# Six windowed attention layers on one NeuronCore: an inverse and a normalization placed earlier in the round

## What is computed

```python
def attn_layer(x, Wqkv, qs, ksc, Wo):              # 16 heads of 64, windows of 32
    q, k, v = split(x @ Wqkv)
    q = l2norm(q) * qs;  k = l2norm(k) * ksc       # row norms: 1/sqrt(sum of squares)
    q = q*cos*scale + rotate_half(q)*sin*scale
    k = k*cos/scale + rotate_half(k)*sin/scale
    attn = softmax(mask(8.0 * q @ k2.T), -1)       # k2, v2: this window and the one before
    return (attn @ v2) @ Wo
for i in range(6):
    x = attn_layer(shift_tokens(x), ...) + x
    x = ffn_layer(shift_tokens(x), ...) + x        # layer norm, gelu gate, two products
```

## Time and profile before

| what | value |
|---|---|
| median of 3 runs (lowest, highest) | 2273.87 us (2270.52, 2282.59) |
| span of the profiled execution, which is its own time here | 2279.7 us |
| TensorE busy | 2005.6 us, 88% |
| VectorE busy | 1815.6 us, 80% |
| ScalarE busy | 1660.3 us, 73% |
| GpSimd busy | 1267.3 us, 56% |

### The profile page before, as it was taken

How to read it: one execution, slowest core, us unless ns; L and a number is a source line. 1 busy time by engine, 2 the same in 40 slices (tenths; PEclk the granted TensorE clock), 3 DMA queues, 4 the chain that set the end, 5 groups by cost and what they waited for, 6 DMA issues and landing times. The chain is left out here.

```text
span 2279.7 us, 55457 instructions
## 1 busy us (share of the span) xinstructions
PE 2005.6 (88%) x20349; PEld 1350.3 (59%) x20349; DVE 1815.6 (80%) x3618; ACT 1660.3 (73%) x3144; POOL 1267.3 (56%) x1132
## 2 busy tenths in 40 slices
PE   5788888689999999999999999999999999985274
PEld 3333333356766776776676767677667767764153
DVE  4666663699999999999999999999999999944633
ACT  2255556378888888888888888888888888874123
POOL 4400000577677777767767766776776776731052
PEclk8699998799999999999999999999999999997587
DMA  6311100111111121111211112111211111100512
GB/s 159 101 42 44 23 2 11 58 36 38 30 39 29 35 82 29 39 29 39 78 29 39 30 41 75 31 37 30 87 30 29 39 30 38 30 29 26 188 34 68
DMA packets 70562, 107.36 MB, mean 47 GB/s; under 512 B 20887, under 2 KB 47774, under 8 KB 68734
## 3 DMA queue, kind: packets, MB, share of 16 engines
q1 hardware_dynamic: 68262, 100.87, 15.4%
q0 software_dynamic: 1280, 2.62, 0.4%
q10 hardware_dynamic: 752, 0.33, 0.1%
HBM read 41.60 MB, written 12.26 MB: 24 GB/s over the span
## 5 line engine op out<-in xcount | busy, mean ns | idle before, releaser
L1583 POOL TENSOR_TENSOR qk<-rot_cos,rot_sin 128x512 f32<-128x512 f32 x256 | 323.2, 1273 | 154.6 <-DVE rot_sin L1361 154.6
L1593 POOL TENSOR_TENSOR qk<-qk,rnorm 128x512 f32<-128x512 f32 x256 | 263.1, 1043 | 88.0 <-DVE rnorm L1394 88.0
L1359 DVE TENSOR_TENSOR rot_cos<-pA,layer_tab 128x512 f32<-128x512 f32 x384 | 263.2, 685 | 60.1 <-ACT sq L1171 55.1
L434 ACT ACTIVATE probs_by_key<-pT 128x512 f32<-128x512 f32 (+3 forms) x384 | 177.1, 490 | 155.4 <-PE pT L320 121.0
L499 DVE TENSOR_REDUCE minus_max<-pS 128x1 f32<-128x1024 f32 (+7 forms) x256 | 184.6, 754 | 110.0 <-PE pS L290 109.2
L1171 ACT ACTIVATE sq<-pA 128x512 f32<-128x512 f32 x384 | 228.5, 595 | 53.1 <-PE pA L890 43.6
L1371 DVE TENSOR_REDUCE sumsq<-sq 128x8 f32<-128x512 f32 x384 | 253.6, 671 | 14.3 <-ACT sq L1171 14.2
L1361 DVE TENSOR_TENSOR rot_sin<-pA,layer_tab 128x512 f32<-128x512 f32 x384 | 261.1, 680 | 0.0
L1231 ACT ACTIVATE probsT<-pD 64x512 f32<-64x512 f32 x380 | 224.0, 589 | 35.3 <-PE pD L931 31.9
L1600 POOL TENSOR_TENSOR probs<-probs,row_inverse 128x1024 f32<-128x1024 f32 x96 | 182.6, 1903 | 100.3 <-DVE row_inverse L1430 100.3
L1191 ACT ACTIVATE qT<-pC 64x512 f32<-64x512 f32 x384 | 225.9, 588 | 7.3 <-PE pC L905 0.5
(11 more groups left out here) (342 smaller groups left out, 4659.0 us busy)
## 6 DMA issues: line engine op xcount, KB each, us to landing
v_shifted<-v SPq DMA_DIRECT2D x96, 384.0 KB, 3.5
v_shifted<-v SPq DMA_DIRECT2D x95, 128.0 KB, 3.4
q_stack<-stacked SPq DMA_DIRECT2D x24, 192.0 KB
k_stack<-stacked SPq DMA_DIRECT2D x24, 192.0 KB
W_ahead<-in_Wqkv_dram SPq DMA_DIRECT2D x12, 384.0 KB
layer_weights<-in_Wqkv_dram SPq DMA_DIRECT2D x12, 384.0 KB
stacked<-part SPq DMA_DIRECT2D x32, 128.0 KB, 2.4
tokens_in<-tokens SPq DMA_DIRECT2D x2, 1024.0 KB
```

The lines of the kernel that those rows point to most:

```text
L1359: dve.tensor_tensor(t1[c % 2][:, :].rearrange("p (h g d) -> p h g d", g=2, d=32), a, tabl[s % 2][:, j].unsqueeze(1).broadcast_to([P, 8, 2, ...
L1583: pool.tensor_tensor(qk(s, c), t1[c % 2][:, :], t2[c % 2][:, :], ALU.add).then_inc(added[c], 1)
L1593: pool.tensor_tensor(v, v, rn[p % 2][:, o:o + 8].unsqueeze(2).broadcast_to([P, 8, DH]), ALU.mult).then_inc(scaled[c], 1)
```

## The change

Two calls move in the hand-written lists. In `dve_body`, `rec(r - 2, 1)` moves from behind `ss(2, r, 1)` to directly behind `sum_(r - 2, 1)`. In `pool_body`, `norm(r - 2, 1)` moves from behind the last two sums of the round's second tile to ahead of them, and those two sums swap places.

```diff
@@ dve_body
             rec(r - 2, 0)
             ss(0, r, 1)
             sum_(r - 2, 1)
+            rec(r - 2, 1)
             ss(1, r, 1)
             rot(1, r, 1)
             rot(2, r, 1)
             ss(2, r, 1)
-            rec(r - 2, 1)
             ya(r - 3)
             ss(3, r, 1)
             nw(r)
@@ pool_body
             norm(r - 2, 0)
             add(0, r, 1)
+            norm(r - 2, 1)
+            add(1, r, 1)
             add(2, r, 1)
-            add(1, r, 1)
-            norm(r - 2, 1)
             sc(1, r, 0)
```

## The result

The changed kernel took 2210.28 us (median of 4 runs, 2202.35 to 2220.80); the kernel before, with one more run, 2272.19 us (2270.23 to 2282.59). The ratio is 0.972, 95% interval 0.967 to 0.976: faster by 62 us, where 50 were forecast. The direction and the mechanism held; the gain was a quarter larger than forecast.

A forecast was written before the change was run, and what follows sets the result against it. Each round was taken as closed by a loop through TensorE, ScalarE and VectorE, with Newton held by GpSimd. 45 rounds x 1.10 us = 49.5 us, with the third round 50 us together: median 2273.87 to 2224 us, range 2209 to 2255.

The forecast's parts named there:

- The overlap with the normalization: VectorE's first Newton instruction is held while GpSimd's second normalization runs: 1.92 us instead of 0.23, 1.69 us a round.
- GpSimd's new chain: GpSimd runs normalization, sum of chunk 0, second normalization, sums of chunks 1 and 2 in succession, ending at 1255.1.
- the 0.8 us of margin: Time between GpSimd going quiet and the start of Newton on VectorE, 0.8 us.
- 0.27 us for the reciprocal's new place: Directly behind its sum the reciprocal delays `ss` and `rot` of chunk 1 by 0.27 us, covered by later idle time.
- What the 1.69 us are worth: Step turning VectorE's saving into round time: TensorE's idle time 0.96 plus 0.14 us, 1.10 us a round.
- My 0.14 us: Share counted of TensorE's 0.23 us wait at a V projection's weight load, a little over half.
- the 0.73 of the prediction: Part of VectorE's 1.69 us that exceeds TensorE's 0.96 us idle time ahead of `W2` and becomes margin, 0.73 us.
- 1 us for the third round: The third round loses its own 1.6 us but gets a new overlap with a sum; about 1 us of gain left.
- Longer waits of VectorE for squares: Sign of being right: VectorE's waits for squares, 1.03 and 0.31 us a round before, grow with TensorE as the bound.
- the first rival: GpSimd's last sum runs into Newton and holds it instead of the normalization; 0.42 us a round remain, 2255; chance 0.10.
- the second: Rival: VectorE was the only bound, so the full 1.69 us a round is gained, 2198; chance 0.04.
- the third or fourth: Rivals: TensorE stops for another wait, 2249 to 2274, chance 0.12; the moved reciprocal delays what follows, 2286, chance 0.05.

## Why the prediction was wrong in size

**What held.** The overlap with the normalization, its 1.69 us, and that it goes (1.924 to 0.226 us); GpSimd's new chain and the 0.8 us of margin; no cost for the other order of the sums; 0.27 us for the reciprocal's new place, fully covered. TensorE as the bound afterwards.

**The step that failed** is "What the 1.69 us are worth": "0.96 + 0.14 = 1.10 us". The measured value is 1.54 us. TensorE's own list takes 31.85 us, and I had taken 32.43 us of its round for work, from its busy time: the limit was the right one and its size was wrong. TensorE's timeline of the kernel before, at the end of a round:

```profile
1261.37 0.44 PE L964 MATMUL pD<-ident,x_feature_major 128*128 128x128 f32 x2
1261.78 1.12 PE L896 MATMUL pA<-layer_weights,x_feature_major 128*128 128x512 f32 x2
1262.75 1.02 PE L890 MATMUL pA<-layer_weights,x_feature_major 128*128 128x512 f32 x2
1263.67 0.63 PE L905 MATMUL pC<-ident,tokens 128*128 128x128 f32 x4
1264.14 1.02 PE L890 MATMUL pA<-layer_weights,x_feature_major 128*128 128x512 f32 x2
1265.00 0.60 PE L905 MATMUL pC<-ident,tokens 128*128 128x128 f32 x4
1266.56 0.67 PE L1062 MATMUL pE<-ff_midT,W_ahead 128*128 128x256 f32 x2 [0.96 <-DVE ff_midT L1474]
```

and of the changed one:

```profile
1200.84 0.44 PE L964 MATMUL pD<-ident,x_feature_major 128*128 128x128 f32 x2
1201.12 1.02 PE L896 MATMUL pA<-W_ahead,x_feature_major 128*128 128x512 f32 x2
1201.98 1.02 PE L890 MATMUL pA<-layer_weights,x_feature_major 128*128 128x512 f32 x2
1202.83 0.60 PE L905 MATMUL pC<-ident,qk 128*128 128x128 f32 x4
1203.27 1.02 PE L890 MATMUL pA<-layer_weights,x_feature_major 128*128 128x512 f32 x2
1204.13 0.60 PE L905 MATMUL pC<-ident,qk 128*128 128x128 f32 x4
1204.57 1.46 PE L1062 MATMUL pE<-ff_midT,W_ahead 128*128 128x256 f32 x6
```

From start to start, before and after: last transposes to `W2` 1.56 and 0.44 us, so this wait was 1.12 us, not 0.96. The recorded duration of four transposes, 0.60 us, is longer than the 0.44 us after which TensorE takes the next thing, and it hid 0.16 us of the wait. `L1` to V projection 0.41 and 0.28; V to Q projection 0.97 and 0.86; Q projection to transposes 0.92 and 0.85; transposes to Q projection 0.47 and 0.44. That is 0.34 us in four steps that the profile calls busy. My 0.14 us stood for the first of them, the V projection's wait (0.13); I had put the rest at nothing. `W2` took 1.37 us until the next transposes started (from 1233.17 to 1234.54 in the same timeline), and takes 1.30 now (from 1204.57 to 1205.87). Together 1.12 + 0.34 + 0.07 = 1.53 us. Much of it could be read before: elsewhere in the old round four transposes are followed after 0.44 us, a Q projection after 0.86 and six matmuls like `W2`'s (L977) after 1.30, and I had not compared them. For the step from the V to the Q projection it could not: the old round shows 0.96 us at its other place too, and why 0.86 is reached now stays open, as it does for `L1`, which has no second place. With less slack than I took, the margin of VectorE came out at 0.19 us and not at the 0.73 of the prediction.

**Two smaller terms.** 43 full rounds at 1.54 us are 66 us; the earlier, shorter rounds and the few longer ones give the other 4 us (forecast 1 us for the third round). Against that stand the several us by which the start of a run scatters, which I had not considered beyond 5 us. That 2210.28 us lies 1 us inside the range of 2209 to 2255 is luck of this kind: two of the four runs took 2202 and 2203 us, and the 70.5 us that the layers gave would make 2202. Of the four only the one at 2217.59 us has a trace, so for the others the start is not shown.

**Signs that I named.** Rounds of 32.3 us: wrong, 31.85. A busy share near 99%: 100%. Longer waits of VectorE for squares: wrong; they are 0.80 and 0.41 us against 1.03 and 0.31, since the round shrank by nearly all that VectorE gave up; my argument against the first rival, that they grow, fails with it. **The rivals:** the first occurred only in the third round of the changed kernel, the 0.617 us in its source line; the second was nearly right, 1.54 of 1.69 us, at a chance of 0.04 that was too low because it rested on the same 32.43 us; nothing of the third or fourth.

## What to carry to other kernels

A small VectorE instruction that takes several times as long as its siblings and ends together with a GpSimd instruction is being held by it; ask what GpSimd runs at that moment, and order its list so that it is idle there. Look at the siblings too, since the hold can move to the next one. Sum the slack of an engine whose recorded ends are modelled from start to start, against the shortest distance of the same forms elsewhere: busy time hid more than a third of it here. And before a term is called bounded by another engine, test by adding a little work, and by taking some away: that gave the limits here to a few hundredths of a us, and showed that they depend on each other.

## What the runs showed of the hardware

A one-input `tensor_scalar` between SBUF tensors in float32 is held by GpSimd as a two-input instruction is (1.90 us against 0.23), while beside GpSimd's multiplications and sums a row sum of 128x1024 takes its 1.20 us, one of 128x512 its 0.63 to 0.68, and the reciprocal its 0.25. The hold is taken instruction by instruction: with GpSimd busy without a gap, one Newton instruction waited out each GpSimd instruction (1.05 and 1.20 us behind two sums, 1.07 and 0.97 us behind two halves) and got its turn ahead of the next. A Newton instruction that started 0.08 us ahead of a 1.90 us multiplication took 0.23 us, and its successor, which takes 0.23 us when it is free, 1.81.
